# Issuing the channel mix of the next round for two chunks at a time in a fused adaLN and LoRA kernel

## The reference

```
h  = einsum('bct,bcd->bdt', x, w_cond[cond])          # a 64x64 channel mix for each sample
x1 = x + h @ W_base.T + b_base                        # a dense 1024x1024 layer
       + sum over the best 2 of 8 experts of route * (h @ A.T) @ B.T     # rank 16
y  = x1 @ w1[adapter].T                               # a 1024x1024 matrix for each sample
out = x1 + 16 * sum over 8 heads of softmax(y @ Wr.T + br) * (y @ A1.T) @ B1.T
```

## Time and profile before

| what | value |
|---|---|
| median of 3 runs | 762.08 us (761.33 to 764.79) |
| the profiled execution's own time | 761.86 us |
| its span, first to last instruction | 760.2 us |
| mean granted TensorE clock | 0.98 of full speed |
| TensorE matmul busy | 720.3 us, 95% of the span |
| VectorE busy | 340.1 us, 45% |
| ScalarE busy | 113.3 us, 15% |

### The profile page before, as it was taken

One profiled execution on the slowest core, in us unless ns is written; L12 is line 12 of the kernel. 1 busy time (PEld: TensorE's weight loads), 2 busy tenths in 40 slices (PEclk: granted clock), 3 DMA queues, 4 the chain that ended last, 5 costly groups with the idle time before them and its releaser, 6 DMA issues.

```text
span 760.2 us, 11873 instructions
## 1 busy us (share of the span) xinstructions
PE 720.3 (95%) x4160; PEld 631.5 (83%) x4160; DVE 340.1 (45%) x877; ACT 113.3 (15%) x307; POOL 54.6 (7%) x113
## 2 busy tenths in 40 slices
PE   5799999999999999999999999999999999999855
PEld 5799988888888988888889888888888888988643
DVE  2300382235634544355436553456345534554554
ACT  1122210111111111111011111111111111110110
POOL 1122210000100000001000100011000100010000
PEclk9999999999999999999999999999999999999966
DMA  8999794027721783169514950487128731764272
GB/s 324 401 374 366 237 376 179 1 93 267 258 109 56 285 315 129 55 209 370 177 56 170 370 214 28 166 314 278 53 100 311 282 115 58 254 231 153 91 286 111
DMA packets 37106, 156.26 MB, mean 206 GB/s; under 512 B 8772, under 2 KB 9796, under 8 KB 26820
## 3 DMA queue, kind: packets, MB, share of 16 engines
q1 hardware_dynamic: 26114, 78.72, 28.0%
q0 software_dynamic: 9216, 71.31, 25.9%
q10 hardware_dynamic: 1730, 5.58, 1.8%
HBM read 133.24 MB, written 22.35 MB: 205 GB/s over the span
## 4 chain that ended last, share of the span: by engine, by line
PE 87%; DMA 5%; SPq 4%; DVE 2%; issue 1%; ACT 0%; POOLq 0%; POOL 0%; DVEq 0%
PE base_ps L308 17%; PE base_ps L310 17%; PE base_ps L309 17%; PE mix_ps L328 7%; PE base_ps L317 6%; PE low_ps L371 4%; PE out_ps L371 4%; DMA adapter<-folded 3%; PE mix_ps L341 3%; SPq L241 1%; PE out_ps L309 1%; PE out_ps L308 1%; PE low_ps L341 1%; PE out_ps L341 1%; PE out_ps L310 1%
## 5 line engine op out<-in xcount | busy, mean ns | idle before, releaser
L308 PE MATMUL base_ps<-yT,w_hi 128*128 128x512 f32 x512 | 203.3, 397 | 0.2
L310 PE MATMUL base_ps<-yT,w_hi 128*128 128x512 f32 x512 | 200.4, 391 | 0.0
L309 PE MATMUL base_ps<-yT,w_lo 128*128 128x512 f32 x512 | 200.2, 391 | 0.0
L595 DVE TENSOR_TENSOR yT<-mix_ps,yT 128x512 fp32r<-128x512 f32 x64 | 44.3, 692 | 164.2 <-ACT yT L486 164.2
L308 PEld LDWEIGHTS base_ps<-yT,w_hi 128*128 128x128 f32 x512 | 96.2, 188 | 22.2 <-DVE xT L706 3.2
L310 PEld LDWEIGHTS base_ps<-yT,w_hi 128*128 128x128 f32 x512 | 96.1, 188 | 20.7
L309 PEld LDWEIGHTS base_ps<-yT,w_lo 128*128 128x128 f32 x512 | 96.3, 188 | 17.4
L317 PE MATMUL base_ps<-ag_raw,stage 128*128 128x136 f32 x640 | 78.4, 287 | 12.8 <-DMA stage<-in_w 12.8
L317 PEld LDWEIGHTS base_ps<-ag_raw,stage 128*128 128x128 f32 x640 | 78.1, 198 | 13.0 <-issue 13.0
L607 DVE TENSOR_TENSOR x1T<-xT,x1T 128x256 fp32r<-128x256 f32 x128 | 48.4, 420 | 71.2 <-ACT x1T L493 71.1
L808 POOL DMA_DIRECT2D adapter<-folded x64 | 34.3, 536 | 596.7 <-PE low_ps L371 517.7
(11 more groups left out here) (120 smaller groups left out, 677.3 us busy)
## 6 DMA issues: line engine op xcount, KB each, us to landing
adapter<-folded POOLq DMA_DIRECT2D x64, 1088.0 KB, 7.0
stage<-in_w SPq DMA_DIRECT2D x40, 512.0 KB, 6.2
x_rows<-in_x SPq DMA_DIRECT2D x32, 512.0 KB, 5.6
xT<-in_x_turned SPq DMA_DIRECT2D x16, 1024.0 KB, 7.8
out<-xT SPq DMA_DIRECT2D x32, 512.0 KB, 2.6
folded<-adapter ACTq DMA_DIRECT2D x10, 544.0 KB, 6.3
w_raw<-in_w SPq DMA_DIRECT2D x8, 256.0 KB, 8.5
w_raw<-in_w SPq DMA_DIRECT2D x4, 512.0 KB, 7.7
```

The lines of the kernel that those rows point to most:

```text
L308: pe.matmul(dst, st_hi, mv_lo, start=start, stop=False, skip_group_check=True)
L309: pe.matmul(dst, st_lo, mv_hi, start=False, stop=False, skip_group_check=True)
L310: return pe.matmul(dst, st_hi, mv_hi, start=False, stop=stop, skip_group_check=True)
L595: dve.tensor_tensor(yT[:, 1, k, :], mix_ps[k % 2][:, :], yT[:, 0, k, :], ALU.subtract).then_inc(yT_lo_done, 1)
```

## The change

In the second pass `mix` is no longer called behind every `base(q, r, 1, k)`. Behind an odd k it is called twice, for chunk k - 1 and for chunk k; behind an even k it is not called.

```diff
                     base(q, r, 1, k)
-                    if ahead:
+                    if ahead and k % 2:
+
+                        mix(q, r + 1, k - 1)
                         mix(q, r + 1, k)
                     if l1 and k == 1:
                         turn_lw(q, r - 1)
```

## The result

The changed kernel takes 785.56 us (median of 4 runs, 782.84 to 789.4) against 761.71 us for the kernel before (4 runs). The ratio is 1.0319 with a 95% interval of 1.0266 to 1.0371. It is 23.9 us slower; the forecast was 786.8 us, with 24.8 us for the change.

What follows compares the result with a forecast made beforehand. TensorE was taken to bound the kernel, its matmuls busy for 95% of the span. 761.86 us plus 18 stalls of 1.38 us (24.8 us) gave 786.7, put at 786.8 us with the runs' median; range 783.5 to 790.5.

Steps and rivals of the forecast that it cites:

- The saving of four changes of kind a pass: TensorE, float32 mixes against other matmuls: four places instead of eight; a pair costs 1.78 us either way, saving 0.
- The chain: Odd steps: mix(k - 1), ScalarE's high part, VectorE's low part, `final`, then `make_out` on TensorE at t + 3.04.
- The stall of 1.38 us: TensorE's wait at `make_out` in steps 3, 5 and 7: 1.35 + 0.12 - 0.09 us, bounds 1.26 to 1.54.
- The bare stall: `make_out` released at t + 3.04 instead of starting at t + 1.69: 1.35 us.
- The two small terms: TensorE at the stall: 0.12 us more for an uncovered weight load, 0.09 us less lost right behind a mix.
- How often: Steps 3, 5 and 7 of six rounds with both layers: 18 stalls, 24.8 us, bounds 22.7 to 27.7.
- the covers: Even steps and the transposed rows' low part in step 2 cost nothing; step 2's margin shrinks from 1.9 to about 1.1 us.
- the cover in even steps: `final` behind the odd chunk's low part ends well ahead of the next `make_out`, which comes at t + 6.5 us.
- Part is given back: Rival: stalls absorb TensorE's idle time at the loop's turn and late adapters, 3.1 us: 783.7 us; chance 0.08.
- Not slower: Rival: pairing makes the mixes cheaper, so the time is 762 to 766 us; chance 0.02.
- The clock falls: Rival: each stall brings 3.4 us at half clock, 1.7 us lost 18 times: 817 us; chance 0.04.
- The signs: Profile: 18 `out_ps` L308 waits of about 1.4 us, 22 to 26 us in all; clock 1.00, matmul busy about 720 us.

Runs made afterwards that it cites:

- the second time: The changed kernel, unchanged, timed once more against the kernel before on the same chip: 785.51 us, ratio 1.0308.
- pairs without a stall: The changed kernel, but VectorE does `final` of chunk k - 2 ahead of the low part of chunk k: 759.89 us, ratio 0.9976; repeated, 759.97 us, 0.9968.

## Why the prediction was right

**What bounds the kernel.** Right: TensorE's stalls added to the time one for one, as far as the scatter lets one see. They are 18 x 1.37 = 24.7 us by the trace; the medians give 23.9 us, and 22.9 the second time, both with 24.7 inside their intervals.

**The saving of four changes of kind a pass, booked at 0.** Right to 0.06 us a round. The stream of pairs without a stall starts `make_out` 1.70 us behind the pair, where 1.69 was worked out, and a round with four pairs is 0.06 us shorter (78.76 against 78.82).

**The chain.** Right, link by link: 1.09, 1.71, 2.32 and 3.05 us against 1.08, 1.71, 2.31 and 3.04. That the queue of VectorE and the one bank make it was shown from both sides: with `final` ahead of the low part it is gone, with 0.36 and 0.89 us more ahead of `final` it grows by 0.35 and 0.89, with a second bank it is gone but for the remainder that was worked out.

**The stall of 1.38 us.** It was 1.37, and not by luck. The bare stall is 3.05 - 1.70 = 1.35 us. The two small terms can be told apart with the run with two banks. Behind the wait, the distance to the next matmul is 225.43 - 225.09 = 0.34 us in the changed kernel, where a mix stands ahead. It is 243.79 - 243.45 = 0.34 us with two banks too, where no mix stands ahead but a product. So a standstill costs 0.34 - 0.227 = 0.11 us whatever went before, where 0.12 was taken for the uncovered weight load; and the 0.09 us that a product loses right behind a mix doesn't come on top, as was assumed. The records put the cost in another place than the prediction did: the matmul starts beside the load, at 225.09, and the next one is late.

The load does start only with the release, as the trace of before had it. What the Trainium skill says (TensorE: Matmul & The Clock Gate, section "Architectural detail"), that the queue can pull weight loads ahead of matmuls in flight, did not hide it. The waiting load starts together with its matmul, at 225.09.

**How often, and the covers.** 18 waits, none in even steps, none for `lwT`. One reading of the cover in even steps was short: by the prediction's times that `final` is done near t + 4.4 us, and it ended at 226.78, or t + 4.74, since the last of the three matmuls ends later than the next can be issued. `make_out` came at 228.62, t + 6.58, and the cover held. The "fifteen products" ahead of it are fifteen matmuls.

**The rivals.** *Part is given back* is refuted for step 7: that stall alone cost 1.36 us in the round that was measured, and 8.2 us for six. *Not slower* fell with the result. *The clock falls* was wrong for this change (1.00 through the loop), but the same stall lengthened to 1.99 us brings it, in seven places of 18, and each costs nearly the 1.7 us that the prediction put on it. The Trainium skill (TensorE: Matmul & The Clock Gate, section "A second HAM failure mode: psum-queue depth-cycling") tells of a kernel in which short idle gaps between groups of matmuls made the clock swing. The traces with waits of 1.99 us agree with it; in those with 1.10 and 1.45 us the clock didn't move.

**The signs.** The matmul busy time was to stay about 720 us and reads 725.0, with the same 4160 matmuls; the records that reach into the stalls make 4.9 us. The recorded waits are 1.10 us each and 19.8 in sum, where about 1.4 and 22 to 26 were named: the prediction gave the stall by starts, and the recorded wait is shorter.

## What to carry to other kernels

A wait that costs nothing today can hang on distance alone: before two pieces of work are moved together, follow the in-order queue of the engine that consumes them, and ask what else stands in it behind the piece that is now late. Here the mix's own waits were satisfied, and the loss came from `final`, which shares nothing with the mix but its place in VectorE's queue. The size can be worked out from one step of the trace before: release time by the chain, less the work that still lies beside it. If the pairs were wanted, the cure would be to put the old work ahead of the new in the consumer's queue (0.9968 of the kernel before, no wait left) sooner than one more bank (1.0032, six short waits left).

## What the runs showed of the hardware

What a stall costs beyond itself depends on its length. With 18 stalls in which TensorE stood still for 1.10 or 1.45 us by the record, none brought the clock down. With 18 of 1.99 us, at the same places, seven stretches of 3.4 us at 1.2 GHz appeared in the loop, in both executions that were profiled, and those that can be read between two stalls cost 1.6 us each. The step from 1.45 to 1.99 us of wait, worth 9.7 us by itself, cost 17. Why the clock fell behind these seven stalls and not behind the other eleven is not shown.

The recorded wait understates a stall. It read 1.10 us where the distance between starts gave 1.37, and 0.40 where a whole round was 0.73 us longer. The record of the matmul ahead reaches past the place at which the next could have started, and the first matmul behind the wait took 0.34 us to the next one instead of 0.227.
